# A gated cross-attention and expert layer on one core: separate PSUM banks for max products and other jobs, 64-row score products, weighted values in mid-step

## The reference

```python
q = (x @ Wq + bq).reshape(B, N, NUM_HEADS, HEAD_DIM)     # x: layer-normed, 4 x 512 x 256
k = (y @ Wk + bk).reshape(B, M, NUM_HEADS, HEAD_DIM)     # y: 4 x 1601 x 192
v = (y @ Wv + bv).reshape(B, M, NUM_HEADS, HEAD_DIM)
scores = jnp.einsum('bnhd,bmhd->bhnm', q, k) * scale
attn = jax.nn.softmax(scores, axis=-1)
out = jnp.einsum('bhnm,bmhd->bnhd', attn, v).reshape(B, N, IMAGE_DIM)
h = jax.nn.relu(out @ W1 + b1)
return h @ W2 + b2
...
x = x + tanh(g_xattn) * attention(layernorm(x), ctx)
x = x + tanh(g_ffn) * experts(layernorm(x))              # shared expert plus the best 2 of 8
```

## Time and profile before

| | before |
|---|---|
| median of three runs | 1354.66 us |
| the profiled execution, span | 1354.8 us |
| TensorE busy in it | 1254.9 us (93%) |
| VectorE, ScalarE busy | 749.8 us, 546.8 us |
| first weighted values, last step's end | 106.6 us, 922 us |

### The profile page before, as it was taken

How to read it: one execution, slowest core, us unless ns; L and a number is a source line. 1 busy time by engine, 2 the same in 40 slices (tenths; PEclk the granted TensorE clock), 3 DMA queues, 4 the chain that set the end, 5 groups by cost and what they waited for, 6 DMA issues and landing times. The chain is left out here.

```text
span 1354.8 us, 16247 instructions
## 1 busy us (share of the span) xinstructions
PE 1254.9 (93%) x5662; PEld 704.1 (52%) x5662; DVE 749.8 (55%) x1624; ACT 546.8 (40%) x1004; POOL 97.3 (7%) x114
## 2 busy tenths in 40 slices
PE   6899999999999999999999999997858999999982
PEld 2455545555645555554555565544434555555551
DVE  1498776686776588576668778632601222222244
ACT  1006564564555366346456547771201111111110
POOL 4000000000000000000000000000170000000044
PEclk9959999999999999899999999997988999999996
DMA  9344403323210453040322421010850111111124
GB/s 308 45 68 71 53 1 47 63 37 51 28 26 1 53 90 49 5 53 1 41 32 34 53 30 24 5 51 4 297 184 31 32 46 40 39 48 39 39 71 124
DMA packets 53840, 78.43 MB, mean 58 GB/s; under 512 B 13312, under 2 KB 38912, under 8 KB 53760
## 3 DMA queue, kind: packets, MB, share of 16 engines
q1 hardware_dynamic: 47744, 67.01, 24.9%
q0 software_dynamic: 3072, 8.39, 1.9%
q10 hardware_dynamic: 2944, 1.98, 0.5%
HBM read 32.47 MB, written 16.52 MB: 36 GB/s over the span
## 5 line engine op out<-in xcount | busy, mean ns | idle before, releaser
L442 ACT ACTIVATE probs<-st_ps 128x512 f32<-128x512 f32 (+1 forms) x832 | 450.5, 598 | 361.8 <-PE st_ps L542 360.6
L677 DVE TENSOR_REDUCE mpart<-ring 128x1 f32<-128x402 f32 x1024 | 521.3, 568 | 85.0 <-PE ring L488 83.0
L488 PE MATMUL ring<-kst,qst 128*128 128x402 f32 x1024 | 389.1, 406 | 0.8 <-DVE xnT L637 0.3
L542 PE MATMUL st_ps<-qst,kst 128*128 128x512 f32 (+1 forms) x832 | 327.7, 400 | 1.9 <-ACT probs L442 1.8
L488 PEld LDWEIGHTS ring<-kst,qst 128*128 128x128 f32 x1024 | 200.1, 196 | 215.1 <-DVE mpart L677 175.9
L554 PE MATMUL pv_ps<-probs,vp 128*17 128x512 f32 (+1 forms) x1664 | 219.6, 600 | 0.1
L542 PEld LDWEIGHTS st_ps<-qst,kst 128*128 128x128 f32 (+1 forms) x832 | 154.0, 187 | 41.8 <-ACT probs L442 19.5
L845 ACT ACTIVATE s_sb<-gu_ps 128x512 f32<-128x512 f32 x55 | 32.9, 598 | 304.8 <-PE gu_ps L920 252.5
L920 PE MATMUL gu_ps<-wgu,xbT 128*128 x312 | 144.1, 604 | 7.4 <-issue 7.3
L1049 DVE TENSOR_TENSOR h_sb<-s_sb,gu_ps 128x512 f32<-128x512 f32 x55 | 37.8, 687 | 204.0 <-ACT s_sb L845 184.0
L920 PEld LDWEIGHTS gu_ps<-wgu,xbT 128*128 128x128 f32 x312 | 56.1, 189 | 78.5 <-issue 78.5
(11 more groups left out here) (125 smaller groups left out, 716.2 us busy)
## 6 DMA issues: line engine op xcount, KB each, us to landing
kst<-parts SPq DMA_DIRECT2D x192, 100.2 KB
qst<-parts SPq DMA_DIRECT2D x192, 32.0 KB
sorted_x<-zeros SPq DMA_DIRECT2D x1, 4992.0 KB, 16.4
xb<-sorted_x SPq DMA_DIRECT2D x39, 128.0 KB, 2.1
sorted_y<-ysb SPq DMA_DIRECT2D x39, 128.0 KB, 1.7
wgu<-in_WgT SPq DMA_DIRECT2D x16, 256.0 KB, 6.7
wgu<-in_WuT SPq DMA_DIRECT2D x16, 256.0 KB, 7.1
wd<-in_WdT SPq DMA_DIRECT2D x8, 512.0 KB, 8.4
```

The source lines that it names most:

```text
L442: nc.scalar.activation(probs[0:w, m % NPB, h, :], st_ps[0:w, (4 * m + h) % NST, :], ACT.Exp, scale=SCALE).then_inc(exp_done, 1)
L488: last = nc.tensor.matmul(slot[:, 0:SCH], qst[u % NKB][:, h, t * P:(t + 1) * P], kst[u % NKB][:, h // 2, score_at(q):score_at(q) + SCH], s ...
L542: nc.tensor.matmul(st_ps[0:w, idx % NST, :], kst[u % NKB][:, h // 2, mt * P:mt * P + w], qst[u % NKB][:, h, :], start=True, stop=True).the ...
L677: last = nc.vector.tensor_reduce(mpart[:, h, t, q:q + 1], slot[:, 0:SCH], AX.X, ALU.max)
```

## The change

- The ring is gone. Chunks have three banks of their own (`s_ps`, `NS`), the weighted values keep theirs, and a tensor of four banks (`work`, `NW`) holds the scores in banks 1 to 3 and every other job of the steps in bank 0; before and after the steps the jobs rotate over all four.
- Scores and chunks read only the 49 or 48 rows of their own head, at row 0 or row 64, so `qst` shrinks to one tile for two heads. Chunks come in pairs, one of either half.
- The order of a step is: first pair, two scores, weighted values, the other pairs, two scores, other jobs. A step has two or three pairs (32 a unit over 13 steps).
- SUM, DIV, W1, W2, XT, Q, K and V stand at other steps (W1 at steps 7, 8, 9, 11 in place of 5 to 8; DIV at 4 in place of 2).
- The K and V products run over 128 rows in both parts: the second operand is padded with zeros in the weights and ones in the data, and the bias of V is row 64 of the padded weights.
- ScalarE takes XT, V and W1 out of PSUM in place of VectorE.
- A stack is loaded by 16 DMAs in place of 28.
- VectorE normalises the next batch's rows at the end of step 0 of a batch's second unit, before the XT jobs.

```diff
-NSLOT = 4
+NS = 3
+NW = 4
...
     def scores(u):
-        return [("S", u, h, t, q) for h in range(4) for t in range(NT) for q in range(4)]
+        return [("S", u, p, t, q) for p in range(2) for t in range(NT) for q in range(4)]
...
+        if u > 0:
+            at[2].append(("SUM", u - 1))
+            at[4].append(("DIV", u - 1))
...
+    def bank(n):
+        return 0 if n in inner else n % NW
...
-                        for g, (qpart, kpart) in enumerate(((0, 0), (0, 1), (1, 0))):
...
+                        both, third = slice(64 * j, 64 * j + 2 * HD), slice(64 * j + 2 * HD, 64 * j + STK)
+                        sp.dma_start(kst[u % NKB][both, p, :].bitcast(F32),
+                                     kc[r:r + HD, dt].bitcast(F32)).then_inc(loaded, 16)
+                        sp.dma_start(qst[u % NKB][both, p, :].bitcast(F32),
+                                     qc[r:r + HD, dt, 0:1, :].to_broadcast([HD, 2, N]).bitcast(F32)).then_inc(loaded, 16)
...
+                elif kind == "V":
+                    _, b, g = job
...
+                    act.wait_ge(job_full, count(job))
+                    nc.scalar.activation(vp[0:w, b % 2, 2 * g:2 * g + mts, :, 0:HD],
+                                         slot[0:w, 0:mts * D].rearrange("p (m h d) -> p m h d", h=H, d=HD), ACT.Copy
+                                         ).then_inc(free_act, 1)
...
+            def score(pair):
+                _, u, p, t, q = pair
+                if (t, q) == (0, 0):
+                    pe.wait_ge(stack_loaded[u % NKB][p], STACK_LOADS * (u // NKB + 1))
+                for j in range(2):
+                    n = 2 * pair_at[pair] + j
+                    rows = slice(64 * j, 64 * j + STK)
+                    if n >= NS:
+                        pe.wait_ge(s_free, n - NS + 1)
+                    nc.tensor.matmul(s_ps[:, n % NS, 0:SCH], qst[u % NKB][rows, p, t * P:(t + 1) * P],
+                                     kst[u % NKB][rows, p, score_at(q):score_at(q) + SCH],
+                                     start=True, stop=True).then_inc(s_full, 1)
...
-                nc.tensor.matmul(st_ps[0:w, idx % NST, :], kst[u % NKB][:, h // 2, mt * P:mt * P + w],
-                                 qst[u % NKB][:, h, :], start=True, stop=True).then_inc(st_full, 1)
+                rows = slice(64 * (h % 2), 64 * (h % 2) + STK + 1)
+                nc.tensor.matmul(work[0:w, 1 + idx % NST, :], kst[u % NKB][rows, h // 2, mt * P:mt * P + w],
+                                 qst[u % NKB][rows, h // 2, :], start=True, stop=True).then_inc(st_full, 1)
...
+            for u, mt, chunk, jobs in steps:
+                for pair in chunk[0:1]:
+                    score(pair)
+                for h in range(2):
                     st(u, mt, h)
-                for job in chunks[4:] + others:
+                if MT * u + mt > 0:
+                    pv(MT * u + mt - 1)
+                for pair in chunk[1:]:
+                    score(pair)
+                for h in range(2, 4):
+                    st(u, mt, h)
+                for job in jobs:
                     do(job)
```

More of the change, by code:

```diff
@@ L91, in schedule, with x_jobs, k_jobs, v_jobs @@
+    def x_jobs(b):
+        return [("XT", b, dt) for dt in range(2)], [("Q", b, dt) for dt in range(2)]
+    def k_jobs(b):
+        return [("K", b, dt, q) for dt in range(2) for q in range(4)]
+    def v_jobs(b):
+        return [("V", b, g) for g in range(VJOBS)]
+    chunks = [[] for _ in range(UNITS * MT)]
+    early = scores(0)
     for u in range(1, UNITS):
-        chunks, start = scores(u), MT * (u - 1) - LEAD
-        for n, chunk in enumerate(chunks):
-            at = start + n * MT // len(chunks)
+        start = MT * (u - 1) - LEAD
+        for n, chunk in enumerate(scores(u)):
+            at = start + n * MT // len(scores(u))
@@ L124, in schedule @@
-        for mt, more in extra.items():
-            jobs[MT * u + mt] += more
-    steps = [(m // MT, m % MT, sorted(jobs[m], key=lambda job: job[0] != "S")) for m in range(UNITS * MT)]
+                for mt, job in zip((3 * n + 5, 3 * n + 6, 3 * n + 7), (("XT2", n, 0), ("XT2", n, 1), ("LG", n))):
+                    at[min(mt, MT - 1)].append(job)
+    xt, q = x_jobs(0)
+    first = k_jobs(0) + xt + q + v_jobs(0)
     b = B - 1
-    epilogue = ([("SUM", UNITS - 1), ("DIV", UNITS - 1)] + [("W1", b, f) for f in range(F1 // P)] +
-                [("W2", b, 0), ("W2", b, 1)])
@@ L131, in schedule @@
-    return prologue, steps, epilogue
+    last = ([("SUM", UNITS - 1), ("DIV", UNITS - 1)] + [("W1", b, f) for f in range(F1 // P)] +
+            [("W2", b, 0), ("W2", b, 1)])
+    return first, early, [(m // MT, m % MT, chunks[m], others[m]) for m in range(UNITS * MT)], last
 def build(nc, I, O):
@@ L452, in do @@
             def do(job):
[L453 to L456 removed]
+                n = place[job]
+                slot = work[:, bank(n)]
+                if n in before_in_bank:
+                    free_bank(before_in_bank[n])
                 kind = job[0]
@@ L710, in do @@
                                                        ).then_inc(x1_ready, 1)
-            for job in prologue:
+            for job in first:
+                if job == ("XT", 0, 0):
+                    normalise(0)
+                    statistics(1)
                 do(job)
-            for u, mt, jobs in steps:
+            for pair in early[:2 * 16]:
+                top_of(pair)
+            do(("MX", 0))
+            for pair in early[2 * 16:]:
+                top_of(pair)
+            for u, mt, chunk, jobs in steps:
+                b, hg = divmod(u, 4)
+                for pair in chunk:
+                    top_of(pair)
                 for job in jobs:
                     do(job)
+                if hg == 1 and mt == 0 and b + 1 < B:
+                    normalise(b + 1)
+                    if b + 2 < B:
+                        statistics(b + 2)
                 if u == UNITS - 1 and mt == 2:
                     second_norm()
-            for job in epilogue:
+            for job in last_jobs:
                 do(job)
```

346 lines of the change are left out of this document (168 added, 178 removed).

## The result

The changed kernel takes 1405.58 us (median of 5, 1402.93 to 1434.13), the kernel before 1353.83 on the same chip: a ratio of 1.0406, 95% interval 1.0355 to 1.0458. Forecast were 1343. A repeat on another chip (e10) gave 1404.65 and 1.0391 (1.0349 to 1.0432). The time lies inside the widest range that was stated, 1290 to 1415, but on the other side of the kernel before than the forecast.

A forecast was written before the change was run, and what follows sets the result against it. The prediction took attention to be bound by the sum of TensorE's instructions. It summed 1354.8 + 3 (attention) - 15 (prologue) = 1343 us, with its own range 1328 to 1360 and a wider one 1290 to 1415.

The forecast's parts named there:

- Two pairs: Plain attention steps with two pairs: 3.02 us becomes 2.87, with weighted values waiting for ScalarE's exponential; -16 in all.
- Three pairs: Attention steps with three pairs: 3.87 us, +0.85, since the fourth chunk waits for VectorE to free a bank; +75 in all.
- Jobs: Attention steps that also hold K, V, Q, W1, W2, SUM, DIV or XT work: shorter, -48 in all.
- Attention +3: All attention steps together: three-pair +75, two-pair -16, steps without chunks +2, jobs -48, W1's waits and low clock -10.
- -10 for W1's waits: Attention steps with a batch's first W1: three waits for packed rows go, with some low clock, -10 us.
- Prologue -15: Before the steps: K products -5, V products -5, a possible clock rise -5; between -9 and -21 us.
- the halves do not run side by side: Rival on pairs in the steps: a pair costs two products, +50 us, 1393; chance 0.13.
- Way out of pv costs less: Rival behind the weighted values: no drain or open weight load, 0.2 less every step, -41, 1302 us; chance 0.12.
- stall is no stall: Rival on three-pair steps: they take 3.05 us instead of 3.87, giving 1271; chance 0.04.
- some low clock: Low-clock time beside the first W1 waits in the steps, counted as going with them within the -10 us.
- the clock falls: Rival on plain steps: TensorE idles more, a third run at 1.2 GHz, 1.1 us each, +76, 1419; chance 0.20.

The follow-up runs named there:

- e12: Changed kernel with products over all 128 rows, taken one by one, one ahead of each score tile: 1337.68 us, ratio 0.9888 to the kernel before.
- e11: Changed kernel with the halves of pairs taken one by one, each ahead of a score tile, still over half rows: 1476.09 us, ratio 1.0860 to before.
- e3: Changed kernel with score and chunk products over all 128 rows again, zeros in the other head's rows: 1359.82 us, ratio 1.0191 to the kernel before.
- e15: Changed kernel plus four VectorE-paced blocks before its first step; second block two full-row products a round (clock rose to 1.00), third one (fell to 0.50).
- e4: Kernel before with only the K and V products padded to 128 rows: 1291.97 us, ratio 0.9686 to the kernel before.
- e14: e12 with its products dealt out singly, five in nearly every step, not four or six: 1325.34 us, ratio 0.9803 to the kernel before.
- e9: e4 with score tiles and products for the maxima over 64 or 65 rows: median 1347.62 us against 1352.51 before, too spread for a ratio.
- e13: Changed kernel plus five unpaced product blocks before its first step; third block 240 products over 48 rows in one half: granted clock 0.50.
- e7: Changed kernel with score tiles over all 128 rows, products for the maxima still over half rows: 1424.8 us, ratio 1.0551 to the kernel before.
- e8: Changed kernel with products for the maxima over all 128 rows, score tiles still over half rows: 1416.48 us, ratio 1.0476 to the kernel before.

## Why the prediction was wrong

By its own steps:

- *Two pairs* 2.87: measured 2.84. *Three pairs* 3.87: 3.77, with the wait for VectorE's bank where it was put. Right.
- *Jobs*: V 1.54 over plain: 1.30. K 1.17: 1.30. W1 1.56: 1.29. SUM and DIV 0.58: 0.37 and 0.47 (steps of 3.21 and 3.31 in e10). Right within 0.3. Q and W2 in two-pair steps were to become 0.17 shorter and became longer: 1.95 and 3.74 over plain, where they were 1.72 and 3.46 before.
- *Attention +3*: this holds -10 for W1's waits. The +3.5 of the medians leaves these out, and the waits of the first XT steps too. W1's waits went and were worth 12; the first XT steps take some 5 more than their kind (1.7 in each of the two that e12 has at full clock). By this estimate the steps are worth about -3 without the clock. Right within its 10, in part by luck: the plain steps came out 12 us below the sum's terms for them, other terms above theirs. *Prologue -15*: -18.6.
- *Rival "the halves do not run side by side"*: refuted (0.46 for two). *"Way out of pv costs less"* and *"stall is no stall"*: refuted by the step times.
- *The step that failed*: the sum priced every step at the upper clock. It put the clock's cost at nothing and even counted "some low clock" as gone, and the rival "the clock falls" got 0.20, since "between the rows, nothing excludes it". It is what happened: 264 us of the steps ran at the lower level, which cost some 80 or more. The rival said a third of the steps and 1.1 us each, +76, 1419. Measured: 54 of 207 steps mostly at the lower level, 1.5 to 1.6 each for plain ones, the steps +82 in the profiled execution and +68 in e10's. It had too many steps and too small a price, so that its sum came near is luck.

What should have tipped it stood in the earlier trace rows: chunks alone, one every 0.48 us, ran at 0.58, steps with scores at 1.00. In the changed plain step four products for maxima and four scores run as four pairs, and a pair takes TensorE as long as one product did; the step is only 0.18 shorter. For scores and maxima its array does about half of the work of the step before in nearly the same time (the weighted values are as before), and stands nearer to the first stretch than to the second. The prediction counted waits ("idle for more of its time"), and for its busy engine went by a share that counts a half-used array as full; e12 against e11, e3 against the changed kernel and e15's second and third block show that the work is what to count.

The other error was to take the parts as one. Padding K and V was worth 0.969 alone (e4), and all else that was taken apart costs: pairs in bunches, 42 us with full rows (e3 to e12); dealing by pairs, 12.5 (e12 to e14); three banks, 12 (argued from e14 against e4); halves, a loss by the clock in three orders (e3 to the changed kernel, e4 to e9, e12 to e11). ScalarE's share, the fewer stack copies and the places of the jobs were not tested one by one.

Open stays why e11's halves one by one lose the clock for 409 us and e9's, in nearly the same order, for 121. In e11 a product for the maxima and the score tile behind it lie in the same half and start 0.30 apart (299.99 and 300.29), where the two of a pair start 0.01 apart. That would fit e13's third block, but no run tested it. Whether halves could pay with the clock held (e9's steps sum to 751 us at the upper level, e4's to 776) wasn't shown either.

## What to carry to other kernels

Before making TensorE's products smaller, ask which engine then sets the step. If it is not TensorE, the array only does less in the same time, and the clock, on which everything else on TensorE depends, can fall to half. Price a tiling change by the array's work per time in the new step, set beside stretches of the old trace with their granted clock, and not by busy time. And take a change apart before judging it: here one part of it alone was worth 3%.

## What the hardware showed that was not expected

- A gapless stream of 48-row products in one half of the array fell to half clock: 0.42 us for 512 columns, against 0.113 per product with both halves in use, which ran at full clock (e13).
- With plain steps of nearly the same length, TensorE busy for 93 to 99% and 98 to 100% of them, products over halves had a granted clock of 0.79 over the steps and products over all rows, zeros included, 0.99 (e11, e12).
- Changing between half rows and full rows at each product cost 0.3 us a change at the lower level (e13), and made a mixed two-pair step (3.14, 3.22) longer than either pure one (2.84 and 3.02; e7, e8).
